# Spreading the softmax reciprocals with fp16 high and low parts, a set-up cut in three, and a new order of all steps

## What is computed

```
qkv = einsum('bcxy,oc->boxy', ln(x), w_qkv) + b_qkv     # 4 heads of 32
q = softmax(q over the head's 32 channels) * scale
k = softmax(k over positions)
context = einsum('bhdn,bhen->bhde', k, v / n)
out = layernorm(w_out @ (context^T q) + b_out) * g_ln
x = x + out
t = tokens(x);  z = layernorm(t)
probs = softmax(z @ router_w + router_b);  top 2, rescaled
y = t + sum over the two experts of p * (z @ expert_w + expert_b)
```

## Time and profile before

| what | value |
|---|---|
| median of 3 runs | 396.46 us (395.44 to 397.31) |
| profiled execution, its own time | 394.62 us |
| its span, first to last instruction | 392.0 us |
| mean granted TensorE clock | 0.948 |
| busy: PE, DVE, ACT, POOL | 80%, 73%, 59%, 55% |

### The profile page before, as it was taken

How to read it: one execution, slowest core, us unless ns; L and a number is a source line. 1 busy time by engine, 2 the same in 40 slices (tenths; PEclk the granted TensorE clock), 3 DMA queues, 4 the chain that set the end, 5 groups by cost and what they waited for, 6 DMA issues and landing times.

```text
span 392.0 us, 7817 instructions
## 1 busy us (share of the span) xinstructions
PE 314.6 (80%) x2896; PEld 186.6 (48%) x2896; DVE 286.0 (73%) x383; ACT 230.9 (59%) x409; POOL 215.0 (55%) x245
## 2 busy tenths in 40 slices
PE   2373888878899999999999999899989898748370
PEld 2271544344347545754575447434743474226250
DVE  1446726564898989898989898989888968437760
ACT  0330495797778667866786678656865775640100
POOL 8311101650488358835883587458725971786470
PEclk9997599999999999999999999999999999997685
DMA  3223030033003412331233003300331030113101
GB/s 75 55 104 96 2 84 0 12 95 91 22 33 91 95 28 57 97 92 27 63 100 85 28 25 89 84 23 25 89 81 27 28 82 24 28 27 80 29 16 38
DMA packets 14805, 21.83 MB, mean 56 GB/s; under 512 B 5310, under 2 KB 5344, under 8 KB 14768
## 3 DMA queue, kind: packets, MB, share of 16 engines
q1 hardware_dynamic: 13558, 19.97, 20.2%
q10 hardware_dynamic: 1210, 1.36, 1.4%
HBM read 4.38 MB, written 4.19 MB: 22 GB/s over the span
## 4 chain that ended last, share of the span: by engine, by line
PE 52%; POOL 12%; ACT 11%; DVE 9%; issue 6%; DMA 3%; SPq 2%; ACTq 1%; POOLq 0%; PEldq 0%; DVEq 0%
PE narrow L968 27%; PE wide L968 13%; PE sums L971 6%; PE small L968 6%; POOL xhat L519 5%; ACT eq L623 3%; DMA x_in<-in_x_dram 2%; DVE kmax L848 2%; POOL low L524 2%; ACT high L602 2%; ACT high L663 1%; POOL paired L504 1%; POOL scaled L509 1%; POOL x L514 1%; ACT squares L649 1%
## 5 line engine op out<-in xcount | busy, mean ns | idle before, releaser
L920 DVE TENSOR_TENSOR gated<-wide,gates 128x1024 f32<-128x1024 f32 x64 | 76.6, 1219 | 23.8 <-PE wide L968 21.8
L504 POOL TENSOR_TENSOR paired<-gated 128x512 f32<-128x512 f32 x64 | 81.4, 1283 | 13.5 <-PE sums L971 7.7
L968 PE MATMUL wide<-w_stack,stack 100*128 100x256 f16 (+1 forms) x512 | 58.7, 259 | 8.4 <-DVE gated L920 6.5
L968 PEld LDWEIGHTS wide<-w_stack,stack 100*128 100x128 f16 x512 | 41.5, 103 | 37.3 <-issue 16.1
L480 POOL TENSOR_TENSOR xhat<-centered,rstd 128x992 f32<-128x992 f32 x8 | 14.9, 1861 | 66.8 <-PE small L968 45.1
L848 DVE TENSOR_REDUCE kmax<-wide 128x1 f32<-128x1024 f32 x32 | 39.1, 1222 | 13.5 <-PE wide L968 12.9
L971 PE MATMUL sums<-ident,paired 128*128 128x128 f32 x256 | 40.0, 290 | 9.4 <-POOL paired L504 8.0
L612 ACT ACTIVATE ek<-narrow,wscale 128x512 f32<-128x512 f32 x64 | 41.2, 685 | 10.7 <-PE narrow L968 8.0
L623 ACT ACTIVATE eq<-narrow,wscale 128x512 f32<-128x512 f32 x64 | 42.4, 687 | 8.3 <-PE narrow L968 7.1
L844 DVE TENSOR_TENSOR eq<-eq,wide 128x1024 f32<-128x1024 f32 x32 | 38.7, 1212 | 7.3 <-PE wide L968 7.3
L837 DVE TENSOR_REDUCE nqmax<-wide 128x32 f32<-128x1024 f32 x32 | 38.3, 1220 | 6.4 <-PE wide L968 5.3
(11 more groups left out here) (146 smaller groups left out, 573.7 us busy)
## 6 DMA issues: line engine op xcount, KB each, us to landing
stack<-high SPq DMA_DIRECT2D x120, 64.0 KB, 2.0
stack<-low SPq DMA_DIRECT2D x60, 64.0 KB, 2.0
out_dram<-y_out SPq DMA_DIRECT2D x15, 256.0 KB
x_in<-in_x_dram SPq DMA_DIRECT2D x7, 512.0 KB
stack<-high ACTq DMA_DIRECT2D x8, 64.0 KB, 2.1
x_in<-in_x_dram SPq DMA_DIRECT2D x1, 256.0 KB
x_in<-in_x_dram ACTq DMA_DIRECT2D x1, 256.0 KB
stack<-low ACTq DMA_DIRECT2D x4, 64.0 KB, 2.1
```

What stands on the lines that cost most here:

```text
L504: nc.gpsimd.tensor_tensor(paired[:, n % PAIREDS, :, :, :], gated[:, n % GATEDS, 0:E // 2, :, :], gated[:, n % GATEDS, E // 2:E, :, :], ALU ...
L920: nc.vector.tensor_tensor(gated[:, n % GATEDS, :, :, :].rearrange("p e t c -> p t e c"), src.rearrange("p (t e c) -> p t e c", t=4, e=E), ...
L968: return nc.tensor.matmul(dst, lhs, rhs, start=start, stop=stop)
```

## The change

Three edits and a new table. First, the spread. `headcols` is scaled by 1/32, so z is a 32nd of the head's sum and its reciprocal 32 times as large; `headrows` is fp16 and has 1/32 where it had 1. Of the 8 equal rows of a head, those in the upper half of a 32-row block (`is_low`) now carry the low part: ACT copies zrec times `is_low` to `zhigh` in fp16, so it is zero in the other rows, and POOL subtracts it from zrec into `zparts` in fp16 (step `zlow`, twice per image). One high and one low row meet in each sum of the matmul, which is now fp16 by fp16. Second, the set-up on DVE is cut in three (`set_up_operands`, `set_up_powers`, `set_up_scales`), with one of the norm sums ahead of the second part. ACT and the matmuls wait for `WEIGHTS_V` instead of the whole set-up; the steps for the bias and the output matrix come last. Third, SP issues six DMAs for expert and router weights instead of ten. Fourth, `PERIOD` goes from 2113 to 2081 and every entry of `AT` is new, so the order on all engines moves.

```diff
-        headrows = sb("headrows", [P, HEADS, DH])
+        headrows = sb("headrows", [P, HEADS, DH], f16)
@@
+            sp.dma_start(w_rows[0:3 * C, hi:NW], router_w.unsqueeze(0).broadcast_to([3, C, E])).then_inc(loaded, 16)
+            sp.dma_start(w_rows[3 * C:3 * C + 2, lo:hi], expert_b.rearrange("e c -> (e c)").unsqueeze(0)
+                         .broadcast_to([2, E * C])).then_inc(loaded, 16)
+            sp.dma_start(w_rows[3 * C:3 * C + 2, hi:NW], router_b.unsqueeze(0).broadcast_to([2, E])).then_inc(loaded, 16)
@@
+            def reciprocal_parts(b, r):
+                pool.wait_ge(zhigh_ready, nth("z", b, r) + 1)
+                if b > 0:
+                    pool.wait_ge(wide_full, wide_turn["bc", b - 1, 2 * r + 1] + 1)
+                nc.gpsimd.tensor_tensor(zparts[:, r, :], zrec[:, r, :], zhigh[:, r, :],
+                                        ALU.subtract).then_inc(zparts_ready, 1)
@@
             def denominators(b, r):
+                if b > 0:
+                    act.wait_ge(zparts_ready, nth("zlow", b - 1, r) + 1)
                 nc.scalar.activation(zrec[:, r, :], src, ACT.Ln).then_inc(narrow_free, 1)
                 act.wait_ge(narrow_free, at + 1)
                 nc.scalar.activation(zrec[:, r, :], zrec[:, r, :], ACT.Exp, scale=-1.0).then_inc(zrec_ready, 1)
+                act.wait_ge(zrec_ready, nth("z", b, r) + 1)
+                nc.scalar.activation(zhigh[:, r, :], zrec[:, r, :], ACT.Copy, scale=is_low[:, 0:1]).then_inc(zhigh_ready, 1)
@@
                 if step == SETUP["act"]:
-                    act.wait_ge(setup_v, SETUP_V)
+                    act.wait_ge(setup_v, WEIGHTS_V)
@@
                 if u % 2 == 0:
-                    pe.wait_ge(zrec_ready, nth("z", b, r) + 1)
+                    pe.wait_ge(zparts_ready, nth("zlow", b, r) + 1)
@@
-                             headrows[rows, :, :].rearrange("p h d -> p (h d)"), zrec[rows, r, :])
+                             headrows[rows, :, :].rearrange("p h d -> p (h d)"), zparts[rows, r, :])
```

More of the change, by code:

```diff
@@ L48 @@
 EKS, GATEDS, PAIREDS, XINS, X2S, STACKS = 4, 3, 2, 4, 3, 3
-SETUP_V = 38
+MADE, MAXIMA_V, DIAGONAL_V, WEIGHTS_V, SETUP_V = 29, 19, 23, 32, 39
 ROWS = 100
-PERIOD, STEPS = 2113, range(45496)
+PERIOD, STEPS = 2081, range(44745)
 AT = {
[L54 to L111, removed]
@@ new lines @@
+    "qexp": (9566, 9591, 9599, 9628, 9631, 9703, 9703, 9725),
+    "xt": (4795, 4871),
+    "z": (9793, 9861),
+    "qrows": (9461, 9564),
+    "attend": (11173, 11256),
+    "var2": (11242, 11268),
+    "cent3": (11303, 11404),
+    "var3": (11371, 11504),
+    "kexp": (10068, 10068, 10228, 10348, 10676, 10869, 10965, 10967),
+    "bc": (10294, 10872, 11114, 11169),
+    "experts": (13714, 13744, 13789, 13841, 14020, 14022, 14229, 14231),
+    "kmax": (9148, 9184, 9401, 9496),
+    "qmax": (9190, 9190, 9274, 9307),
@@ new lines @@
+    "xc": (8441,),
+    "router": (12562,),
+    "krow": (9718,),
+    "sums": (10734, 10738, 10921, 10965, 10968, 10968, 11005, 11029),
+    "mix": (11071,),
+    "out": (13878, 13968, 14173, 14176, 14334, 15263, 15419, 15759),
+    "root1_act": (14596,),
+    "high3": (19461, 19748),
+    "high1": (16631,),
+    "e2": (20950,),
+    "logit_act": (20781,),
+    "qexp_act": (17490, 18075, 18085, 18085, 18085, 18169, 18173, 18513),
+    "xt_act": (12528, 12563),
+    "square1": (12783,),
+    "z_act": (18566, 18600),
@@ new lines @@
+    "qrows_act": (17318, 17448),
+    "attend_act": (18886, 18952),
+    "var2_act": (18914, 18968),
+    "cent3_act": (19108, 19171),
+    "var3_act": (19130, 19364),
+    "kexp_act": (18649, 18649, 18653, 18655, 18739, 18739, 18739, 18741),
+    "vsum1": (15549,),
+    "context": (20695,),
+    "mixed": (20946,),
+    "kadd": (20081,),
+    "y": (24342, 25971),
+    "bc_dve": (20345, 20504, 21239, 21300),
+    "experts_dve": (23763, 23763, 24168, 24255, 24255, 24277, 24384, 24477),
+    "kmax_dve": (19333, 19375, 19520, 19553),
@@ new lines @@
+    "kred": (19819,),
+    "qmax_dve": (19378, 19443, 19499, 19502),
+    "low1": (18406,),
+    "route": (22474, 22474, 22474, 22474, 22575, 22665, 22973, 22973, 23375, 23478, 23478, 23478),
+    "qparts": (25302, 25305),
+    "kparts": (25633,),
+    "zlow": (25938, 25966),
+    "gates": (28546,),
+    "pairs": (29613, 29904, 29984, 30090, 30118, 30140, 30140, 30177),
+    "low3": (27484, 27486),
+    "xhat3": (27483, 27483),
+    "x2": (26054, 26129),
+    "scale1": (21818,),
+    "fill3": (14717,),
@@ L112 @@
+    "fill1": (10580,),
+    "store": (18275, 20245),
+    "load": (4404,),
 }
-SETUP = {'transposes': 10766, 'diagonal': 13490, 'operands': 0, 'scales': 19378, 'act': 20541}
+SETUP = {'transposes': 4872, 'diagonal': 8442, 'operands': 0, 'powers': 15550, 'scales': 18407, 'act': 17490}
 def build(nc, x, w_qkv, b_qkv, w_out, b_out, g_ln, router_w, router_b, expert_w, expert_b, out):
@@ L200, in build @@
         zrec = sb("zrec", [P, R, RT])
+        zhigh = sb("zhigh", [P, R, RT], f16)
+        zparts = sb("zparts", [P, R, RT], f16)
+        is_low = sb("is_low", [P, 1])
         squares2 = sb("squares2", [P, R, RT])
@@ L535, in _ @@
                     pair_experts(b, u)
+                for b, r in due("zlow", step):
+                    reciprocal_parts(b, r)
                 for b, r in due("low3", step):
@@ L981, in set_up_maxima @@
             def set_up_maxima():
[L982 removed]
+                pe.wait_ge(setup_v, MAXIMA_V)
                 tr(sums[0:3, 0:P], amax[:, :], ident[:])
```

69 lines of the change are left out of this document (37 added, 32 removed).

## The result

| | before | after |
|---|---|---|
| median of 20 runs | 394.54 us (392.06 to 399.5) | 398.92 us (396.36 to 406.1) |
| profiled execution, span | 392.0 us | 395.3 us |
| mean granted TensorE clock | 0.948 | 0.906 |

The ratio is 1.0105, 95% interval 1.0077 to 1.0133. Medians are of all executions, ratios leave out those that ran over 1.5% above the fastest of their kernel. The forecast was 379.2 us in a range of 372 to 389, with a chance of 0.04 for slower. The measured median lies 9.9 us above that range, and the sign was wrong.

What follows compares the result with a forecast made beforehand. PE was taken to bound the period, with DVE close behind. Seven periods -10.1, start -4.2 and end -3.0 sum to -17.3 against 394.62, or 377.3; with 1.84 for the median, 379.2 us, range 372 to 389.

Steps and rivals of the forecast that it cites:

- PE's gaps can then be from 1.2 us ... I take 2.1: PE's idle time per full period: 1.2 to 3.7 us possible, 2.1 taken, giving a period of 37.2, a gain of 1.57.
- The spread on PE: PE's spread matmuls per image: 2.24 us in fp32 falls to 0.84 in fp16, a gain of 1.40.
- What is added for it: Per image, ACT gets two copies at 0.618 us and POOL two subtractions at 1.160, hidden by other PE work.
- Both reciprocals with their copies now stand ahead of all eight `kexp` drains ... this part is on the path.: On ACT, the reciprocals and copies precede the key drains that `sums` waits for; the start was charged +2.2 us.
- Image 1's load lands at 18.8: At the start, four fewer SP issues save 3.3 us, so image 1 lands at 18.8 instead of 22.1.
- seven small steps ... 1.6: At the start on DVE, seven small steps that stood ahead of the scaling, about 0.2 us each, take 1.6.
- the loads don't land earlier: Rival at the start: image 1 still lands at 22.1, 3.3 us are missing, total 382.5; chance 0.08.
- With both reciprocals and copies ahead of the key drains I get 15.7.: At the start, from the last maximum to the last `sums`: 15.7 us, where it was 13.5.
- `y` held by a store that queues behind a load on SP: Named as a possible wait recurring in each image that would make the forecast wrong; no size given.
- The end, "-3.0": From the last `sums` to the router: 27.1 us instead of 30.2, then nearly the same order, so 3.0 less.
- The rivals: Five: gaps close as well (0.15), period stays (0.17), loads don't land earlier (0.08), longer reciprocal decides (0.05), GpSimd holds VectorE (0.03).
- The routing step L906: DVE step taking 1.95 us beside POOL's `scale1`; in the new order it should be near 0.42.

Runs made afterwards that it cites:

- experiment 5: Changed kernel with image load behind the two stores, plus matmuls nothing reads where PE waited in images 0, 1 and 7: 388.71 us, 0.981 of the kernel before.
- experiment 8: Changed kernel with load behind stores, image 5's second store later, and unread matmuls in more of PE's waits: 386.06 us, 0.974 of the kernel before.
- experiment 3: Also called stores first: changed kernel with the image load moved behind the two stores on SP; 395.09 us, 1.0006 of the kernel before.
- experiment 6: Changed kernel with load behind stores, and image 5's second store moved behind image 6's first: 392.52 us, 0.986 of the kernel before.
- experiment 1: Changed kernel with the spread back in fp32, without ACT's copy, POOL's subtraction and the low rows: 407.66 us, 1.034 of the kernel before.

## Why the prediction was wrong

The forecast for the span was 17.3 us below before; it came 3.3 above. The 20.6 us between them, by the steps of the prediction:

- **"PE's gaps can then be from 1.2 us ... I take 2.1".** Right: 2.10.
- **The spread on PE, "a gain of 1.40".** Right in kind, mis-sized. The 64 matmuls took 9.9 us and not 7. In a full period the spread was busy for 1.2 where before had 2.3, and PE's whole load fell by 0.73. Where the rest of the 1.1 went, no run shows. The period is therefore 37.85 and not 37.2: 0.65 in each of the full ones, 3.1 with the light ones.
- **"What is added for it", ACT's copy 0.618, POOL's subtraction 1.160.** 0.722 and 1.161. The subtraction was hidden in full periods, as said.
- **"Both reciprocals with their copies now stand ahead of all eight `kexp` drains ... this part is on the path."** Seen, and priced as ACT's time alone. What failed is the step from a wait to its price: I took each matmul's length from the earlier trace rows, at the full clock, and never asked what the clock does behind a wait. In period 1 the gain of 1.2 didn't come even with the clock held (36.34), and the clock cost 3.5 (experiments 5, 8): 4.7. Of six profiles with these two waits unfilled, five lost that much and one lost 1.5 (37.82).
- **"Image 1's load lands at 18.8", "seven small steps ... 1.6".** The first is the step that failed in the start, 2.5 us: it took four issues fewer on SP for an earlier landing. The nine profiles that issue six weight loads ahead of the image began its issue anywhere from 10.91 to 12.46 and saw it land (read from the start of PE's work on it) from 20.98 to 22.82, with one of the earliest issues (10.94) landing last; the four with ten loads issued it from 11.88 to 12.73 and saw it land from 21.42 to 22.17. So SP's queue was mostly free earlier, by 1.7 us here, and no gain at the landing stands out from the scatter. That is the rival "the loads don't land earlier", held at 0.08. What sets the landing is open. (The small steps were a slip in the sum: seven at 0.2 are 1.4.)
- **"With both reciprocals and copies ahead of the key drains I get 15.7."** From the last maximum to the last `sums` it took 18.3, or 2.6 more. With the waits filled it took 16.6 and 17.0 (experiments 5 and 8, which are alike in this stretch), so the half clock is 1.3 to 1.8 of it. The start as a whole gained only 0.5 in experiment 5 because its load landed 1.1 later. The rest I put down to the two waits behind the reciprocals (1.42 and 1.59 us again in image 0); no experiment took them apart.
- **The full periods.** "`y` held by a store that queues behind a load on SP" stood in the prediction's last sentence with no price. It came once in each profile with the old place of the load, in period 4: 2.66 us (experiment 3).
- **The end, "-3.0".** It was +1.9, or 4.9 off. The half clock from the first `attend` on and a store beside the last stack copies account for 4.0: with both mended the end is 62.89, 2.0 below before. Fillers alone brought 2.9 against stores first (experiment 5). At equal clocks the late store is worth 1.1 to 1.4 (experiment 6), and the larger part is the clock's.
- **The rivals.** Each was a wait or a cover at full clock; none had the half clock. The routing step L906 behaved as said (now 0.41), while the `gap` of the routing went from 0.19 to 1.28 beside the scaling in full periods. The Trainium skill (GPSIMD Engine Reference, section 8, Key points) has VectorE and GpSimd contend when the VectorE instruction has two SBUF inputs, as the `gap` subtraction has; the trace agrees, at 1.1 us in a period.

With these repairs the kernel is 2.6% faster than before, where the forecast had 4.4%. How much of that is the new arithmetic and order alone isn't shown, since the kernel before got no fillers in its own waits. But 5.5 of the 7.7 us of span lie in the seven periods, which run at clock 1.00 in both kernels.

## What to carry to other kernels

When an order puts a chain of one engine ahead of the work that others wait for, look at the images that have no other work to lay beside it (the first and the last), and price there not only the wait but also the half clock behind it: behind 1.4 and 1.6 us of waiting it cost 3.5 more in five profiles of six. Follow each buffer through its store, not only its load: a store behind a load that waits for something late is a wait of the writer. Two changes that each lose (by 3.4% and 4.7%) lost less together (1%), and gained once the waits and the stores were mended, so neither "one part alone" tells what the other is worth.

## What was not expected of the hardware

- The granted clock fell behind two waits of 1.42 and 1.59 us with one short matmul group between them, behind waits of 0.67 and 0.84 us in experiment 1, and behind single waits of 1.65 us in some executions and not in others: 37.56 or 38.90 us for the same period. Kernels with filled waits scattered by 1.1 and 3.8 us over six runs and 2.4 over twelve, stores first by 6.2 over twelve.
- Matmuls that compute nothing made a period 3.46 us shorter, and the same ones made another kernel's period 2.1 us longer.
- A pair of fp32 matmuls with 32 rows costs as much time alone as four in different row blocks together, 1.06 and 1.07 us (experiment 1); of fp16 a pair took 0.32 from its start to the next work.
- The DMA with the experts' biases as a broadcast source took 2.88 us to issue in one profile, 3.60 and 4.60 in others, where the ten plain ones of the kernel before took 0.42 to 2.00. With six issues SP came to image 1's load at 10.91 to 12.46, with ten at 11.88 to 12.73.
- With the loads of weights and image 1 in either order, the last of them landed at 20.6 to 21.4 us.
